# Earlier scores, a begun attention stage and six stack loads in a fused cross-attention and ternary-FFN kernel

## The chip, the cores and the metric

One core of one Trainium2 chip runs the whole program. The metric is device microseconds (us) of one execution, the median of the runs taken; lower is better. Where a profiled execution is read, times count from the start of its span.

## The reference, cut to what matters

Four sequences of 512 rows. Cross-attention with 32 heads of 16 channels: `q = layernorm(x) Wq`, `k, v = ctx Wkv`, rotary turn of q and k, softmax of `q k / 4`, weighted v, `Wout` and bias, added to x. Then an FFN on a second layer norm: weights become ternary, `sign(round(w / (mean|w| + 1e-6)))` times the mean, rows are quantised to 128 steps, gelu between the two products, added again. The scores must keep fp32 accuracy: q and k are each split in three bf16 parts, and a score is six products of parts (q0k0, q1k0, q2k0, q0k1, q1k1, q0k2) summed in one matmul over 96 stacked rows.

```python
logits = jnp.einsum('bqhd,bkhd->bhqk', q, k) * scale
w = jax.nn.softmax(logits, axis=-1)
attn = jnp.einsum('bhqk,bkhd->bqhd', w, v)
gamma = jnp.mean(jnp.abs(w))
return jnp.sign(jnp.round(w / (gamma + EPS))) * gamma
```

## The kernel before, in words

Every engine has its program written out by hand, in `xattn_ffn` (L1160); order is kept by semaphores alone.

**Projection.** Sixteen tiles of 128 rows, in steps s = 3 to 18. A step of TensorE: turn a tile of ctx and of x, turn the rotated k of the tile before, `project_k`, `project_v`, turn the rotated q, `project_q` (each product in high and low parts, L281). VectorE multiplies by the rotary tables (`rope_products`, L394 to L396) and takes rests (`take_first`, L404), ScalarE copies and splits (L466, L471), GpSimd adds and makes the third part (L502, L506). The parts go to HBM (`store_parts`, L235, twelve transfers for two tiles).

**Early scores.** The row maxima of groups 0 and 1 (a group is 4 heads of one sequence, 32 groups in all) are found within the projection: 32 single scores (`early_scores`, L672) go through one PSUM bank, each read by VectorE (`early_maxima`, L731) before the next is made. Three per step from s = 10; numbers 27 to 31 come behind the last step. Then `add_totals` (L314) and on VectorE `weigh_ffn` (L326) make the FFN's thresholds, four small operations and one more for `gamma_128`.

**Attention.** `tensor_step` (L710) s runs `scores` of group s (maxima by `row_maxima`, L736), `scores_turned` of group s - 2 (its exponentials by `exponentials`, L755), and `weigh_v` of group s - 2, a chunk late. A group's scores need its stacks: 96 rows of q parts and of k parts in SBUF, 4 KB a row, in four slots (`load_stacks`, L573). They need them whole, since `scores` waits for all of them ahead of its first matmul (L657). Group 0's first turned score waits for the last products and rests of the projection at once (L687 to L690).

**The way of a maximum.** GpSimd negates and splits a group's maxima (`split_maxima`, L765), SP turns them with a DMA (`turn_max`, L587) and loads them as two rows below the q stack (`load_max`, L594). `scores_turned` waits for that.

**SP's queue.** All DMAs are issued by SyncE's queue, in the order written. In attention, per SP step s (it falls into `tensor_step` s - 1): `turn_max(s-2)`, `load_stacks(s)`, `load_max(s-2)`, `load_weight(s)`, `pack_sums` (stores a group's sums; every other step `load_quotients`, L633), `turn_weight(s-2)`.

**GpSimd in attention.** `stage_v`, `split_maxima`, `ternarise` of an FFN weight piece (L780, three operations), `divide`.

A stack is loaded by seven transfers, the tuples being (first sixteenth of the target, part, parts):

```python
(mem.q_stack, mem.q_parts, ((0, 0, 3), (3, 0, 2), (5, 0, 1))),
(mem.k_stack, mem.k_parts, ((0, 1, 1), (1, 0, 1), (2, 0, 1), (3, 0, 3))),
```

Two other transfers matter below. `load_quotients` reads 8 blocks of 16 rows of 2 KB (L637, L638) and 8 rows of 2 KB, each repeated 16 times (`unsqueeze(1).to_broadcast([8, 16, 512])`, L639), into 128 partitions. `load_max` writes 2 partitions.

Of the kernel before, what the change touches and what calls it, by code (L numbers as in the profile page):

```python
# [16 lines left out]
HEADS, HEAD = 32, 16  # L17
# [22 lines left out]
STACK_LOADS = DMA * 7  # L40
# [63 lines left out]
class Project:  # L104
# [165 lines left out]
    def product(self, pe, out, lhs, slot, rhs, low_ready, done, high=None, low=None):  # L270

        count = rhs[0].shape[1]
        for a, b in ((0, 0), (0, 1), (1, 0)):
            if a == 1:
                pe.wait_ge(*low_ready)
# [22 lines left out]
    def project_q(self, pe, n):  # L298
# [4 lines left out]
        self.product(pe, self.in_bank[1], self.xT, n % 2, self.wq_sb, (self.x_low_ready, n + 1), self.projected[1],  # L303
                     high, low)
# [21 lines left out]
    def weigh_ffn(self, dve):  # L326
        mem = self.mem
        dve.wait_ge(self.total_ready, 1)
        dve.tensor_scalar(mem.gammas[:], self.total_bank, 1.0 / (FFN * DIM), None, ALU.mult).then_inc(self.gamma_step, 1)
        dve.wait_ge(self.gamma_step, 1)  # L330
        dve.tensor_scalar(self.gamma_eps[:], mem.gammas[:], FFN_EPS, None, ALU.add).then_inc(self.gamma_step, 1)
        dve.wait_ge(self.gamma_step, 2)
        dve.tensor_scalar(mem.limits[:, 0], self.gamma_eps[:], 0.5, None, ALU.mult).then_inc(self.gamma_step, 1)
        dve.tensor_scalar(mem.limits[:, 1], self.gamma_eps[:], -0.5, None, ALU.mult).then_inc(self.gamma_step, 1)
# [146 lines left out]

    def weight_high_too(self, pool, loaded, high, raw, ready):
# [27 lines left out]
class Attend:  # L510
# [3 lines left out]
    SINGLES = EARLY * GH * CHUNKS  # L514
    ST_BANKS = 3

    def __init__(self, nc, mem, prj, sem):
# [8 lines left out]
        self.inverse = slots(late.take(2 * SEQ), 2)  # L526
        self.v_ones = late.take(2 * CHUNKS * GH * 2 * HEAD).rearrange("p (s c h e) -> p s c h e", s=2, c=CHUNKS, h=GH)
        self.raw = slots(late.take(2 * DIM), 2)
# [41 lines left out]

    def load_stacks(self, sp, g):  # L573
        mem, slot = self.mem, g % STACK_SLOTS
# [3 lines left out]
        for stack_sb, where, runs in (  # L578
            (mem.q_stack, mem.q_parts, ((0, 0, 3), (3, 0, 2), (5, 0, 1))),
            (mem.k_stack, mem.k_parts, ((0, 1, 1), (1, 0, 1), (2, 0, 1), (3, 0, 3))),  # L580
        ):
            src = where[g].rearrange("t (d h) c -> (t d) (h c)", h=GH)
            for to, part, count in runs:
                sp.dma_start(stack_sb[to * HEAD:(to + count) * HEAD, slot].rearrange("p h c -> p (h c)"),  # L584
                             src[part * HEAD:(part + count) * HEAD]).then_inc(self.stacks_loaded[slot], DMA)
# [95 lines left out]
    def scores_turned(self, pe, g, k):  # L681
# [15 lines left out]
    def weigh_v(self, pe, g, c):  # L697
        pe.wait_ge(self.exp_done, g * 16 + GH * (c + 1))
        if c == 0:
            pe.wait_ge(self.v_staged, g + 1)  # L700
            if g == 0:
# [7 lines left out]

    def tensor_step(self, pe, s):  # L710
        turned, before = s - 2, s - 3
        for c in range(CHUNKS):
            if 0 <= turned < GROUPS:
                self.scores_turned(pe, turned, 4 * c)
            if s < GROUPS:
                self.scores(pe, s, 2 * c)
            if 0 <= turned < GROUPS:
# [8 lines left out]
            if s < GROUPS:  # L726
# [53 lines left out]
    def ternarise(self, pool, n):  # L780
        w, limits = n % 2, self.mem.limits
        if n == 0:
# [9 lines left out]
                           ).then_inc(self.ternary_ready, 1)  # L792

# [366 lines left out]
def xattn_ffn(nc, x, ctx, pos, wq, wkv, wout, bout, w_fc, w_proj, out):  # L1160
    with ExitStack() as stack:
# [5 lines left out]
        att = Attend(nc, mem, prj, sem)  # L1167
        rows = Rows(nc, mem, att, sem)
# [5 lines left out]
        def _(sp):  # L1174
# [4 lines left out]
            for s in range(TILES + 6):  # L1179
# [5 lines left out]
                if s == TILES + 4:  # L1185
                    sp.wait_ge(prj.projected[1], TILES)
                    att.load_weight(sp, w_fc, w_proj, 0)
                    att.load_weight(sp, w_fc, w_proj, 1)
                if within(s - 5, TILES) and (s - 5) % 2 == 1:
# [6 lines left out]
            for pair in range(2):  # L1196
                sp.wait_ge(prj.parts_stored[pair], PAIR_STORES * BATCH)
# [44 lines left out]
        def _(pe):  # L1242
# [7 lines left out]
            for s in range(3, TILES + 3):  # L1250
                if 2 <= s - 2 < TILES:
# [7 lines left out]
                if s >= 10:  # L1259
                    att.early_scores(pe, 3 * (s - 10))  # L1260
# [4 lines left out]
                if s >= 10:  # L1265
                    att.early_scores(pe, 3 * (s - 10) + 1)
                if within(s - 3, TILES):
                    prj.project_q(pe, s - 3)
                if s >= 10:
                    att.early_scores(pe, 3 * (s - 10) + 2)  # L1270
# [23 lines left out]
        def _(dve):  # L1294
# [17 lines left out]
            for s in range(3, TILES + 3):  # L1312
                if within(s - 4, TILES):
                    prj.rope_products(dve, s - 4, 1)
                if s > 10:
                    att.early_maxima(dve, 3 * (s - 11) + 2)
# [5 lines left out]
                if s >= 10:  # L1322
                    att.early_maxima(dve, 3 * (s - 10))
# [4 lines left out]
                if s >= 10:  # L1328
# [206 lines left out]
```

## Time and profile before

| what | us |
|---|---|
| median of 3 runs | 794.77 (794.23 to 797.53) |
| the profiled execution | 797.79 |
| its span | 795.9 |
| PE busy (matmuls; ends are modelled) | 768.5 |
| DVE busy | 674.4 |
| ACT busy | 456.1 |
| POOL busy | 341.0 |

PE is TensorE's matmul side, PEld its weight loads, DVE VectorE, ACT ScalarE, POOL GpSimd, SP SyncE; a q behind the name is the engine's queue. L12 is line 12 of the kernel before. A row of a timeline has the start, the duration, and in brackets the idle time before it with what ended that. Matmuls are pipelined, so the duration of one isn't the distance to the next.

### The profile page before, as it was taken

What the parts mean: (1) busy time and instruction counts of PE and PEld (TensorE: products, weight loads), DVE (VectorE), ACT (ScalarE), POOL (GpSimd) and SP (SyncE); (2) the same over time, 40 slices, a digit from 0 to 9 for tenths busy, and PEclk for the clock granted to TensorE, in tenths of its full rate; (3) what the DMA queues carried; (4) which work ended last, traced back from release to release, by engine and by line L of the source; (5) the groups of instructions that cost most, each with busy time, mean ns of one, the idle gap of its engine ahead of it and who ended that gap; (6) DMA issues with size and microseconds to landing.
All of it is one profiled execution on the core that took longest, in us unless ns stands there. A gap on an engine that the chain in (4) does not pass through costs nothing.

```text
span 795.9 us, 11662 instructions
## 1 busy us (share of the span) xinstructions
PE 768.5 (97%) x3812; PEld 331.6 (42%) x3812; DVE 674.4 (85%) x945; ACT 456.1 (57%) x811; POOL 341.0 (43%) x445
## 2 busy tenths in 40 slices
PE   4899999799999999999999999999999999999998
PEld 3688877233333222323322222244444444444443
DVE  7788998688888888888888888269999999898895
ACT  5677776477777777767777777734322333223430
POOL 4688777743454455445445544623222121110001
PEclk9999999699999999999999999999999999999999
DMA  8488897535577769796887996326456654555545
GB/s 288 127 216 241 256 254 184 129 109 137 147 141 152 154 158 142 152 171 149 146 155 180 171 176 137 82 57 137 107 110 144 132 106 93 108 117 87 112 87 137
DMA packets 178861, 117.22 MB, mean 147 GB/s; under 512 B 119746, under 2 KB 150514, under 8 KB 178802
## 3 DMA queue, kind: packets, MB, share of 16 engines
q1 hardware_dynamic: 178802, 116.49, 65.7%
q8 instruction: 30, 0.49, 0.3%
q14 instruction: 29, 0.24, 0.1%
HBM read 64.50 MB, written 25.43 MB: 113 GB/s over the span
## 4 chain that ended last, share of the span: by engine, by line
PE 86%; DMA 6%; DVE 3%; SPq 2%; POOL 1%; issue 1%; ACT 1%; POOLq 0%; ACTq 0%
PE banks L967 14%; PE banks L952 14%; PE banks L706 13%; PE banks L692 12%; PE banks L281 11%; PE banks L667 11%; PE banks L938 7%; DMA stack_words<-max_rows 4%; DMA max_rows<-max_parts 2%; PE banks L310 2%; SPq L584 1%; PE banks L678 1%; DVE maxima L740 1%; DMA attn_words<-in_x_dram 1%; ACT probs_words L760 1%
## 5 line engine op out<-in xcount | busy, mean ns | idle before, releaser
L760 ACT ACTIVATE probs_words<-banks 128x512 f32<-128x512 f32 x512 | 272.1, 598 | 101.7 <-PE banks L692 101.0
L740 DVE TENSOR_REDUCE maxima<-banks 128x2 f32<-128x1024 f32 x240 | 283.4, 1216 | 45.6 <-PE banks L667 45.5
L692 PE MATMUL banks<-stack_words 98*128 98x512 bf16 x512 | 175.4, 386 | 4.8 <-DMA stack_words<-max_rows 3.4
L667 PE MATMUL banks<-stack_words 96*128 96x512 bf16 x480 | 144.9, 383 | 0.0
L706 PE MATMUL banks<-probs_words,late_words 128*32 128x512 f32 x1024 | 137.3, 608 | 0.7
L952 PE MATMUL banks<-ternary_words,late_words 128*128 128x512 f16 x512 | 113.1, 380 | 0.0
L967 PE MATMUL banks<-ternary_words,stack_words 128*128 128x512 f16 x512 | 112.9, 380 | 0.0
L1130 ACT ACTIVATE probs_words<-probs_words,h_moments 128x2048 f32<-128x2048 f32 (+1 forms) x17 | 32.2, 1901 | 135.4 <-DVE h_moments L1027 135.4
L692 PEld LDWEIGHTS banks<-stack_words 98*128 98x128 bf16 x512 | 39.8, 98 | 150.0 <-ACT probs_words L760 109.9
L771 POOL TENSOR_SCALAR neg_max<-maxima 128x16 f32<-128x16 f32 x32 | 8.3, 258 | 163.0 <-DVE maxima L740 161.2
L967 PEld LDWEIGHTS banks<-ternary_words,stack_words 128*128 128x128 f16 x512 | 49.9, 98 | 64.4 <-issue 6.6
L952 PEld LDWEIGHTS banks<-ternary_words,late_words 128*128 128x128 f16 x512 | 50.0, 98 | 61.5 <-issue 1.7
L1153 POOL TENSOR_SCALAR h_powers<-h_moments 128x1 f32<-128x1 f32 x16 | 5.5, 342 | 153.4 <-DVE h_moments L1027 153.4
L667 PEld LDWEIGHTS banks<-stack_words 96*128 96x128 bf16 x480 | 47.4, 99 | 56.7 <-issue 1.9
L1124 ACT ACTIVATE probs_words<-banks,row_scale 128x512 f32<-128x512 f32 x64 | 42.3, 682 | 27.5 <-PE banks L952 27.5
L938 PE MATMUL banks<-v_words,attn_words 128*128 128x512 f32 x128 | 57.7, 593 | 0.0
L786 POOL TENSOR_SCALAR late_words<-late_words,limits 128x512 f16<-128x512 f32 x32 | 50.1, 1566 | 0.3 <-POOL late_words L791 0.2
L788 POOL TENSOR_SCALAR late_words<-late_words,limits 128x512 f16<-128x512 f32 x32 | 50.2, 1570 | 0.0
L506 POOL TENSOR_TENSOR ternary_words<-attn_words,ternary_words 128x512 bf16<-128x512 f32 x32 | 37.3, 1166 | 24.3 <-ACT ternary_words L471 23.5
L706 PEld LDWEIGHTS banks<-probs_words,late_words 128*32 128x32 f32 x1024 | 20.2, 108 | 54.9 <-ACT probs_words L760 50.3
L502 POOL TENSOR_TENSOR attn_words<-attn_words 128x512 f32<-128x512 f32 x32 | 41.2, 1290 | 2.2 <-DVE attn_words L396 2.0
L1022 DVE BATCH_NORM_STATS2 h_stats<-probs_words 128x6 f32<-128x512 f32 x64 | 39.4, 679 | 0.0
(139 smaller groups left out, 962.5 us busy)
## 6 DMA issues: line engine op xcount, KB each, us to landing
o_rows<-late_words SPq DMA_DIRECT2D x32, 256.0 KB, 3.3
k_parts<-ternary_words SPq DMA_DIRECT2D x48, 128.0 KB, 3.2
q_parts<-ternary_words SPq DMA_DIRECT2D x48, 128.0 KB, 2.5
stack_words<-q_parts SPq DMA_DIRECT2D x32, 192.0 KB, 3.1
stack_words<-k_parts SPq DMA_DIRECT2D x96, 64.0 KB, 2.7
stack_words<-k_parts SPq DMA_DIRECT2D x32, 192.0 KB, 2.7
attn_words<-in_x_dram SPq DMA_DIRECT2D x16, 256.0 KB, 4.4
probs_words<-in_L_ffn_w_fc_dram SPq DMA_DIRECT2D x16, 256.0 KB, 3.7
```

The lines of the kernel that those rows point to most:

```text
L281: mm = self.nc.tensor.matmul(out, lhs[a][:, slot, k * P:(k + 1) * P], rhs[b][:, k, :], start=(a + b + k == 0), stop=(a == 1 and k == count ...
L667: mm = self.nc.tensor.matmul(self.score_slot[j % 2][:, i], self.mem.q_stack[0:STACK, slot, head, c * P:(c + 1) * P], self.mem.k_stack[0:ST ...
L692: self.nc.tensor.matmul(self.st_bank[(g * 16 + k) % self.ST_BANKS], self.mem.k_stack[0:STACK + 2, slot, head, c * P:(c + 1) * P], self.mem ...
L706: mm = self.nc.tensor.matmul(self.pv_bank[32 * j:32 * j + 32], self.v_ones[:, g % 2, c, j, :], self.probs[:, c, j, :], start=(c == 0), sto ...
L740: dve.tensor_reduce(self.maxima[:, g % 2, 2 * j:2 * j + 2], self.score_slot[j % 2], AX.X, ALU.max).then_inc(self.scores_read, 1)
L760: act.activation(self.probs[:, c, head, :], self.st_bank[(g * 16 + k) % self.ST_BANKS], ACT.Exp, scale=1 / math.sqrt(HEAD)).then_inc(self. ...
L786: pool.tensor_scalar(self.below[:], self.raw[:, w], limits[:, 1, w:w + 1], None, ALU.is_lt).then_inc(self.cut, 1)
L788: pool.tensor_scalar(self.ternary[:, w], self.raw[:, w], limits[:, 0, w:w + 1], None, ALU.is_gt).then_inc(self.cut, 1)
L938: mm = self.nc.tensor.matmul(self.y_bank[n % 2], att.attnT[:, n // CHUNKS * KX + k, c * P:(c + 1) * P], self.wout_sb[:, k, :], start=(k == ...
L952: mm = self.nc.tensor.matmul(self.fc_bank[o], self.uT[:, n % U_SLOTS, part * KX + k], self.fcT[:, k, o], start=(k + part == 0), stop=(k == ...
L967: mm = self.nc.tensor.matmul(self.proj_bank[r], self.hT[:, r, part, k], self.projT[:, k // 2, k % 2], start=(k + part == 0), stop=(part == ...
L1124: act.activation(self.h[:, n % H_SLOTS, o * DIM:(o + 1) * DIM], self.fc_bank[o], ACT.Gelu, scale=self.row_scale[:, n % U_SLOTS]).then_inc( ...
```

## The change

- Early scores start at step 9, with 2, 3, 3, 3, 3, 4, 4, 4, 3, 3 in the ten steps; all 32 lie within the projection. The fourth of a step (in the last step the third) stands inside `project_q`, ahead of its last four matmuls.
- Attention is begun ahead of the last turn of q: the first two scores of group 2 and the first two turned scores of group 0; each of the first three turned scores waits only for what its own PSUM bank held. ScalarE takes the two exponentials between its last projection copies, and loads its table for Exp a step earlier.
- The thresholds are made on GpSimd. Its two `stage_v` and the setting of pads come earlier; group 2's maxima are split between its first two `ternarise`.
- SP: the maxima of groups 0 and 1 are turned and loaded earlier; the stacks of group 4 stand ahead of group 2's maxima; from group 5 on `load_q`, then `load_max`, then `load_k`.
- A stack takes six loads. The k stack becomes k0 three times, k1 twice, k2 once, each by one load with a repeated source; the q stack stays.

```diff
-STACK_LOADS = DMA * 7
+STACK_LOADS = DMA * 6
+    FIRST_STEP = 9
+    PER_STEP = (2, 3, 3, 3, 3, 4, 4, 4, 3, 3)
...
-    def load_stacks(self, sp, g):
+    def load_q(self, sp, g):
...
+        src = self.mem.q_parts[g].rearrange("t (d h) c -> (t d) (h c)", h=GH)
+        for to, count in ((0, 3), (3, 2), (5, 1)):
+            sp.dma_start(self.mem.q_stack[to * HEAD:(to + count) * HEAD, slot].rearrange("p h c -> p (h c)"),
+                         src[0:count * HEAD]).then_inc(self.stacks_loaded[slot], DMA)
+
+    def load_k(self, sp, g):
+        slot = g % STACK_SLOTS
+        for part, to, count in ((0, 0, 3), (1, 3, 2), (2, 5, 1)):
+            src = self.mem.k_parts[g, part].rearrange("(d h) c -> d (h c)", h=GH)
+            sp.dma_start(self.mem.k_stack[to * HEAD:(to + count) * HEAD, slot].rearrange("p h c -> p (h c)"),
+                         src.unsqueeze(0).to_broadcast([count, HEAD, GH * SEQ])).then_inc(self.stacks_loaded[slot], DMA)
...
-            pe.wait_ge(self.prj.multiplied[1], TILES)
-            for side in range(2):
-                pe.wait_ge(self.prj.rest_done[side], TILES)
+            pe.wait_ge(*((self.prj.multiplied[1], TILES), (self.prj.rest_done[0], TILES), (self.prj.rest_done[1], TILES))[k])
...
+    def begin(self, pe):
+
+        self.scores(pe, self.EARLY, 0)
+        self.scores(pe, self.EARLY, 1)
+        self.scores_turned(pe, 0, 0)
+        self.scores_turned(pe, 0, 1)
...
             for s in range(GROUPS + 3):
-                if 1 <= s - 2 < GROUPS:
+                if s == 2:
+                    for pair in range(2):
+                        sp.wait_ge(prj.parts_stored[pair], PAIR_STORES * BATCH)
+                if s == 3:
+                    att.load_stacks(sp, STACK_SLOTS)
+                    att.turn_max(sp, 2)
+                    att.load_max(sp, 2)
+                if 3 <= s - 2 < GROUPS:
                     att.turn_max(sp, s - 2)
-                if STACK_SLOTS <= s < GROUPS:
-                    att.load_stacks(sp, s)
-                if 1 <= s - 2 < GROUPS:
+                if STACK_SLOTS + 1 <= s < GROUPS:
+                    att.load_q(sp, s)
+                if 3 <= s - 2 < GROUPS:
                     att.load_max(sp, s - 2)
+                if STACK_SLOTS + 1 <= s < GROUPS:
+                    att.load_k(sp, s)
...
             prj.turn_rotated(pe, TILES - 1, 0)
-            att.early_scores(pe, 27)
+            att.begin(pe)
             prj.turn_rotated(pe, TILES - 1, 1)
-            for i in range(28, att.SINGLES):
-                att.early_scores(pe, i)
...
             prj.take_first(dve, TILES - 1, 0)
-            att.early_maxima(dve, 27)
             prj.sum_ffn(dve)
-            att.early_maxima(dve, 28)
+            att.row_maxima(dve, 2, 0)
             prj.take_first(dve, TILES - 1, 1)
-            for i in range(29, att.SINGLES):
-                att.early_maxima(dve, i)
-            prj.weigh_ffn(dve)
...
+            att.set_pads(pool, 1)
+            att.stage_v(pool, 1)
+            prj.weigh_ffn(pool)
+            pool.tensor_scalar(rows.gamma_128[:], mem.gammas[:], 1 / Q_B, None, ALU.mult).then_inc(rows.gamma_set, 1)
+            att.ternarise(pool, 0)
+            att.split_maxima(pool, 2)
+            att.ternarise(pool, 1)
```

## Rows read from the trace of the kernel before

**Rows 1.** The page: line 4's shares of the chain, and the turned scores' group.
```profile
PE 86%; DMA 6%; DVE 3%; SPq 2%; POOL 1%; issue 1%; ACT 1%; POOLq 0%; ACTq 0%
L692 PE MATMUL banks<-stack_words 98*128 98x512 bf16 x512 | 175.4, 386 | 4.8 <-DMA stack_words<-max_rows 3.4
```

**Rows 2.** Busy time by stretch: span, length, PE, PEld, DVE, ACT, POOL (count), clock, DMA share, GB/s.
```profile
59.63:66.70 7.07, 7.07 (x39) 5.95 (x39) 5.61 (x14) 5.60 (x13) 5.90 (x8) 1.00 0.61 161
...
97.48:105.23 7.75, 7.75 (x42) 6.17 (x42) 7.29 (x16) 5.59 (x13) 5.86 (x8) 1.00 0.99 282
138.30:147.57 9.27, 4.40 (x17) 1.88 (x17) 6.60 (x12) 3.69 (x5) 4.97 (x6) 0.73 0.76 183
147.57:161.96 14.39, 14.39 (x58) 4.03 (x58) 10.08 (x12) 8.21 (x15) 10.59 (x11) 0.70 0.34 64
161.96:173.31 11.35, 11.35 (x66) 3.48 (x65) 9.93 (x9) 8.47 (x17) 5.32 (x7) 1.00 0.55 160
...
298.52:311.05 12.53, 11.51 (x65) 3.32 (x64) 11.12 (x11) 9.10 (x18) 6.55 (x8) 1.00 1.15 158
```

**Rows 3.** Timeline of the handover on DVE and POOL, and of PE's weighing in the next step.
```profile
138.53 0.69 DVE L394 TENSOR_TENSOR attn_words<-banks,ternary_words 128x512 f32<-128x512 f32 x1 [1.06 <-PE banks L281]
...
139.97 1.26 POOL L502 TENSOR_TENSOR attn_words<-attn_words 128x512 f32<-128x512 f32 x1 [0.60 <-DVE attn_words L396]
...
140.40 0.68 DVE L404 TENSOR_TENSOR attn_words<-banks,ternary_words 128x512 f32<-128x512 f32 x1
...
165.76 1.06 PE L706 MATMUL banks<-probs_words,late_words 128*32 128x512 f32 x8
```

**Rows 4.** PE's busy time and clock before and after the clock falls.
```profile
139.00:142.50 3.50, 1.43 (x8) 1.00 0.81 211
142.60:156.20 13.60, 10.90 (x29) 0.50 0.52 118
```

**Rows 5.** Timeline of SP's queue and of PE while group 0's stacks are loaded.
```profile
63.58 1.81 SPq L584 DMA_DIRECT2D stack_words<-k_parts  x4
...
66.10 0.38 PE L310 MATMUL banks<-ident,attn_words 128*128 128x128 f32 x2
```

**Rows 6.** Timeline of SP's queue in an attention step; PE's first score of the next.
```profile
371.57 1.12 SPq L592 DMA_TRANSPOSE max_rows<-max_parts  x1
372.80 1.44 SPq L584 DMA_DIRECT2D stack_words<-q_parts  x3
374.28 1.81 SPq L584 DMA_DIRECT2D stack_words<-k_parts  x4
376.14 0.70 SPq L596 DMA_DIRECT2D stack_words<-max_rows  x1
...
380.62 0.59 PE L667 MATMUL banks<-stack_words 96*128 96x512 bf16 x2
```

**Rows 7.** DMA issues: KB each, us from issue to landing where it is told.
```profile
stack_words<-k_parts SPq DMA_DIRECT2D x96, 64.0 KB, 2.7
...
late_words<-inverse_rows SPq DMA_DIRECT2D x16, 256.0 KB
...
max_rows<-max_parts SPq DMA_TRANSPOSE x32, 2.4
stack_words<-max_rows SPq DMA_DIRECT2D x32, 8.0 KB
```

**Rows 8.** Timeline of SP's queue: the quotients of a pair.
```profile
228.56 0.65 SPq L638 DMA_DIRECT2D late_words<-o_rows  x1
229.25 0.61 SPq L639 DMA_DIRECT2D late_words<-inverse_rows  x1
```

**Rows 9.** Busy time while they move; the last two columns are DMA share and GB/s.
```profile
232.50:233.50 1.00, 1.00 (x6) 0.43 (x5) 1.00 (x3) 1.00 (x3) 1.00 (x2) 1.00 0.51 193
```

**Rows 10.** The chain of waits in order of time, in a step behind quotients.
```profile
301.03 5.18 DMA max_rows<-max_parts
306.23 4.77 DMA stack_words<-max_rows
```

More of the change, by code:

```diff
@@ L274, in product @@
             if a == 1:
+                if between is not None:
+                    self.att.early_scores(pe, between)
                 pe.wait_ge(*low_ready)
@@ L526, in __init__ @@
         self.inverse = slots(late.take(2 * SEQ), 2)
+        self.raw = slots(late.take(2 * DIM), 2)
         self.v_ones = late.take(2 * CHUNKS * GH * 2 * HEAD).rearrange("p (s c h e) -> p s c h e", s=2, c=CHUNKS, h=GH)
-        self.raw = slots(late.take(2 * DIM), 2)
         self.below = late.take(DIM // 2, F16)
@@ L569, in __init__, with early_of @@
         self.divided = sem("divided")
-    def load_stacks(self, sp, g):
-        mem, slot = self.mem, g % STACK_SLOTS
+    def early_of(self, s):
+        at = s - self.FIRST_STEP
+        if not 0 <= at < len(self.PER_STEP):
+            return []
+        first = sum(self.PER_STEP[:at])
+        return list(range(first, first + self.PER_STEP[at]))
+    def load_q(self, sp, g):
+        slot = g % STACK_SLOTS
         for pair in range(2):
@@ L577, in load_stacks @@
         need(sp, self.st_ready, (g - STACK_SLOTS + 1) * 16)
[L578 to L585, printed above, removed]
+        src = self.mem.q_parts[g].rearrange("t (d h) c -> (t d) (h c)", h=GH)
[3 more added lines that the diff above has]
+    def load_k(self, sp, g):
+        slot = g % STACK_SLOTS
+        for part, to, count in ((0, 0, 3), (1, 3, 2), (2, 5, 1)):
+            src = self.mem.k_parts[g, part].rearrange("(d h) c -> d (h c)", h=GH)
+            sp.dma_start(self.mem.k_stack[to * HEAD:(to + count) * HEAD, slot].rearrange("p h c -> p (h c)"),
+                         src.unsqueeze(0).to_broadcast([count, HEAD, GH * SEQ])).then_inc(self.stacks_loaded[slot], DMA)
+    def load_stacks(self, sp, g):
+        self.load_q(sp, g)
+        self.load_k(sp, g)
     def turn_max(self, sp, g):
@@ L712, in tensor_step @@
         for c in range(CHUNKS):
-            if 0 <= turned < GROUPS:
+            begun = s == self.EARLY and c == 0
+            if 0 <= turned < GROUPS and not begun:
                 self.scores_turned(pe, turned, 4 * c)
-            if s < GROUPS:
+            if s < GROUPS and not begun:
                 self.scores(pe, s, 2 * c)
-            if 0 <= turned < GROUPS:
+            if 0 <= turned < GROUPS and not begun:
                 self.scores_turned(pe, turned, 4 * c + 1)
@@ L725, in tensor_step @@
                 self.scores_turned(pe, turned, 4 * c + 3)
-            if s < GROUPS:
+            if s < GROUPS and not begun:
                 self.scores(pe, s, 2 * c + 1)
@@ L1250, in _ @@
             for s in range(3, TILES + 3):
+                early = att.early_of(s)
                 if 2 <= s - 2 < TILES:
@@ L1258, in _ @@
                     prj.project_k(pe, s - 3)
-                if s >= 10:
-                    att.early_scores(pe, 3 * (s - 10))
+                if len(early) > 2:
+                    att.early_scores(pe, early[0])
                 if 1 <= s - 3 < TILES:
@@ L1321, in _ @@
                     prj.take_first(dve, s - 4, 0)
-                if s >= 10:
-                    att.early_maxima(dve, 3 * (s - 10))
+                if len(early) > 2:
+                    att.early_maxima(dve, early[0])
                 if s < TILES:
@@ L1411, in _ @@
                     prj.normalise(act, s - 1)
+                if s == TILES + 3:
+                    att.exponentials(act, 0, 0)
                 if within(s - 4, TILES):
@@ L1419, in _ @@
                     prj.first_part(act, s - 4, 1)
+                    if s == TILES + 3:
+                        att.exponentials(act, 0, 1)
                     prj.second_part(act, s - 4, 1)
+                if s == TILES + 2:
+                    act.preload_act_table(ACT.Exp)
             for s in range(2, GROUPS + 3):
-                for k in range(16):
+                for k in range(2 if s == 2 else 0, 16):
                     if within(s - 2, GROUPS):
```

84 lines of the change are left out of this document (48 added, 36 removed).

## The prediction

> **What bounds the kernel now.** I read the page first. TensorE holds 86% of the chain that ended last, DMAs 6% [rows 1]. The page's group of turned scores shows where DMAs enter: of 4.8 us that TensorE idles ahead of them, 3.4 us are waits for `load_max`. Then the table by stretch [rows 2]. A projection step takes 7.07 us without early scores and 7.75 us with three, TensorE busy throughout, VectorE 7.29 us of it. A steady attention step takes 11.35 us, again TensorE throughout, with VectorE at 9.93, ScalarE at 8.47 and GpSimd at 5.32. Between the two lies the handover: from the end of the last product (138.3) to the start of the second attention step (161.96) are 23.7 us, with TensorE busy 4.40 us of the first 9.27, while the five late scores go back and forth with VectorE. There the clock falls: behind 3.5 us in which TensorE was busy 1.43, the granted clock is half for 13.6 us [rows 4]. So two things can be won, the handover and 3.4 us of waits; a step of attention can only be lost.
>
> **The handover.** The work that remains behind the last product: VectorE's rotary products start 0.2 us after it, GpSimd's sum ends at 141.23, 2.9 us after it [rows 3]. Then one behind another a turn on TensorE, ScalarE's copy, VectorE's rest (0.68), a turned score and two exponentials: six operations, 0.65 each by the rest's row, 3.9 us. The first weighing of v starts so 6.8 us after the product. In a steady step it starts 3.8 us in (165.76 against 161.96), 7.55 us before the step's end. Sum 14.35 against 23.7: 9.3 us to win at full clock. `turn_rotated` of q stands behind `begin` on TensorE, whose second turned score waits for VectorE's rest of k: products from 138.53, rest 0.68, so 140.6, before GpSimd's 141.23; nothing lost.
>
> Against it stands what moves into the projection. Before the last product's end lay 26 early scores, now 32: six more by (7.75 - 7.07) / 3 = 0.23 us, 1.4 us. Two of the steps with four maxima keep their statistics: VectorE 7.29 + 0.68 = 7.97 of 7.98 us. The score inside `project_q` then waits for the maximum before it; I take 0.3 us each, 0.6 us (bounds 0 and 1.4, two maxima). The first early score of step 9 meets the stacks of group 0: TensorE reaches it at 66.4, and the k loads are issued from 63.58 [rows 5]. Its wait hangs on the k loads: 63.58 + 2.7 - 0.2 + 5.5 = 71.6 by the price below, less the 0.4 taken off there, a wait of 4.8 us; about 1.0 if they move as now (the third, issued near 64.6, lands 2.7 later). At full clock 9.3 - 1.4 - 0.6 - 4.8 leaves a gain of 2.5 us. The clock may fall in that wait or in the handover; it costs step one now at most 14.39 - 11.35 = 3.0 us. I take 1.5 and 0.5 for the later landing of group 4's stacks, on which the turn of group 2's maxima is queued: handover 0.5 us won.
>
> The thresholds leave VectorE for GpSimd, ahead of its first `ternarise`; GpSimd idles half of each step [rows 2], and only the loads of weight pieces wait for it. I cost this, the pads, the two early `stage_v` and ScalarE's earlier table load at nothing. Without that cover it is the four operations' length on GpSimd once, about 1 us.
>
> **The six loads.** This is the term that decides. A step's q and k loads are all issued one step ahead of use. In the step shown [rows 6] the turn is issued at 371.57, q at 372.80, k at 374.28, `load_max` at 376.14, and the scores that need all the loads start at 380.62. The change puts `load_max` (0.70) ahead of k; k is issued from 375.03. That alone costs nothing: a k load lands 2.7 us after its issue [rows 7], by 379.
>
> But the new k loads have a repeated source, three blocks of 16 rows and two blocks of 16 rows, the repeat outermost. What does an outermost extent of 8 do now? The quotients' two transfers [rows 8] have one, and while they move, the 16 DMA engines are busy to 0.51, 193 GB/s in all [rows 9]: eight engines, 23.7 GB/s each. The table of issues gives no landing for these, nor for `load_max` with its 2 partitions, while all that have 16 or more rows outermost have one [rows 7]: the profile counts sixteen engines' completions, and these have fewer. So I expect three engines for the first k load and two for the second, and the second on two of the same, as the two quotient transfers share theirs. On those two lie 32 rows of 4 KB, 131 KB each, 131 / 23.7 = 5.5 us, where sixteen engines take 0.2 us for a 64 KB load.
>
> The Trainium skill, page DMA: Bandwidth & Descriptors, section "Why a DMA increments its semaphore by 16 and not by 1", says that a DMA uses the largest number of engines up to 16 that divides the outermost extents of both sides, and the lowest-numbered ones; the trace agrees for the extent 8 with its share of 0.51. By the rule the sum is the forecast; without it, the rival below.
>
> The price: 375.03 + 2.7 - 0.2 + 5.5 = 383.0 against 380.62, a stall of 2.4 us. The median of 2.7 includes waiting behind other transfers, so I take 2.0. Behind quotients the turn itself takes 5.18 us [rows 10], not 2.4, which puts k later; but a stretched step gives the quotients more time to drain, so I take 2.0 there too. Bounds 0.9 (landing 1.1 earlier) and 3.5. Groups 5 to 31 are 27: 54 us (24 to 95). The 3.4 us of waits for `load_max` go, since its rows land first. What is late next is k; scores, maxima and the next turn follow it, so nothing later absorbs the stall.
>
> **Sum.** 797.8 (profiled execution, span 795.9) - 0.5 - 3.4 + 54 = 847.9. That execution lies 3.0 above the median of the runs, 794.77; I forecast **845 us**.
>
> **Rivals.** (1) **The repeated loads spread over all sixteen engines**, as one with 16 or more rows does. Then k lands by 379, the stack wait of step 9 is 1.0, the handover wins 9.3 - 1.4 - 0.6 - 1.0 = 6.3 us, less up to 3 for the clock, and some 2 of the 3.4 us of waits go: 794.8 - 6.3 - 2 = 786.5 to 790, faster. It decides where the k loads land less than 5.6 us after issue. For it: their target has 48 and 32 rows; against: the quotients' target has 128 and they use eight. (2) **The two repeated loads use different engines**: 64 KB on each, 2.8 us. Odd steps then land at 380.3 and stall no more, even ones by under 1 us: 794.8 - 5 + 13 x 0.5 = 796, no change. Against it: the quotients' share of eight with two transfers in flight. (3) **The clock halves in the stalls**: 2 us of idle in a step resemble the 1.43 of 3.5 of rows 4. Half the clock for 3 us costs 1.5 us a step, in half of the steps 20 us: 865. For it, the fall seen; against, the step from 298.52, with 1.02 of 12.53 us idle, stays at full clock [rows 2].
>
> **Chances.** Forecast 0.65, (3) 0.12, (1) 0.18, (2) 0.05. Slower by over 0.5% (which is what a measurement of this kernel can tell from no change) 0.77, within 0.05, faster 0.18. The forecast's own range is 815 to 886, from the bounds of the stall. Since slower holds less than 8 in 10, the range reaches into (1): 789 to 886.
>
> **What would show it.** Right: the issue rows of the two repeated k loads give no landing; TensorE's waits ahead of L667's successor name the stacks, some 2 us a step; steps of 13 us; DMA share near 2/16 while k moves; TensorE idle near 66 us. The handover shown right: the second attention step starts some 14 us after the last product. Wrong: steps stay at 11.35, k lands within 3 us with a landing told. Then (1) holds and the end is below 791.

## The result, and the profile after

The changed kernel takes **879.17 us** (median of 6 runs, 875.69 to 883.23); the kernel before took 796.85 on the same chip (794.23 to 798.62). The ratio is 1.104, with an interval of 1.100 to 1.108: slower by 82 us. The forecast was 845, with a range of 789 to 886. Direction and place were right; the sum is 34 us short, and the way it was counted was wrong, as the experiments show. One run of the last experiment, the profiled one, took 991.37 us at a granted clock of 0.755; its median below is over the other five runs, and its trace isn't read.

The page of the profiled execution (880.1 us, span 878.3): shares of the chain that ended last, the groups of scores and of turned scores (busy, mean ns | idle before, releaser), and the issues of DMAs (KB each, us to landing where it is told).

```profile
PE 66%; DMA 16%; SPq 7%; DVE 3%; POOL 3%; ACT 2%; issue 2%; POOLq 0%; DVEq 0%; ACTq 0%
...
L689 PE MATMUL banks<-stack_words 96*128 96x512 bf16 x480 | 151.9, 399 | 50.8 <-DMA stack_words<-k_parts 50.8
L712 PE MATMUL banks<-stack_words 98*128 98x512 bf16 x512 | 183.6, 403 | 4.0 <-DVE attn_words L401 1.6
...
stack_words<-q_parts SPq DMA_DIRECT2D x32, 192.0 KB
stack_words<-k_parts SPq DMA_DIRECT2D x32, 192.0 KB
...
stack_words<-k_parts SPq DMA_DIRECT2D x32, 128.0 KB
stack_words<-k_parts SPq DMA_DIRECT2D x32, 64.0 KB
max_rows<-max_parts SPq DMA_TRANSPOSE x32, 3.3
```

Against [rows 1], TensorE's share of the chain falls from 86% to 66% and DMA's rises from 6% to 16%. The scores, which waited for nothing worth a place among the rows of before, idle 50.8 us, all for the k loads; of the waits for the maxima's rows ahead of L712 one of 0.8 us is left. Against [rows 7], the k loads have no landing any more, and the turn of the maxima takes 3.3 us instead of 2.4 (with plain k loads, experiment 1, it takes 3.0, so the repeated loads are not all of that).

The table by stretch of the changed kernel, with the columns of [rows 2]: step 9; handover up to group 0's first turned score; attention's first step; three steady steps; and one microsecond in which TensorE stands still.

```profile
62.41:80.95 18.54, 9.67 (x41) 7.60 (x39) 6.21 (x13) 5.73 (x13) 7.34 (x9) 0.72 0.80 200
...
151.60:153.14 1.54, 1.31 (x10) 0.59 (x7) 1.50 (x4) 1.28 (x2) 1.37 (x5) 1.00 0.09 28
153.14:168.25 15.11, 13.23 (x59) 4.02 (x60) 9.58 (x11) 9.83 (x18) 9.53 (x13) 0.77 0.66 167
208.78:220.12 11.34, 11.34 (x65) 3.42 (x64) 9.93 (x9) 8.46 (x17) 5.32 (x7) 1.00 0.36 103
220.12:236.41 16.29, 13.10 (x65) 3.46 (x64) 10.41 (x10) 8.52 (x17) 5.37 (x7) 0.90 0.79 115
236.41:247.76 11.35, 11.35 (x66) 3.42 (x64) 9.93 (x9) 8.46 (x17) 5.32 (x7) 1.00 0.39 100
...
222.00:223.00 1.00, 0.00 (x0) 0.00 (x0) 0.00 (x0) 0.00 (x0) 0.86 (x3) 1.00 0.17 54
```

The steps don't take 13 us each, as forecast. In most pairs one of 11.35 alternates with one of 16 to 19. In the last row little but k moves. Of its 54 GB/s, 45 go in packets of 4 KB, which is a row of k; summed from the trace, these keep 2.0 of the 16 DMA engines busy, with 22 GB/s each, near the 23.7 of the quotients' eight [rows 9]. Most of the rest of the share of 0.17 is short packets of 256 bytes.

The trace also keeps the completions that each load counts on its semaphore. A group's six loads make 71 of them. Where every load has 16 or more rows outermost, each makes 16; that is 48 for q and 16 for the last k load, so 7 are left for the two repeated loads. The quotients' two loads, with 8 outermost, make 9 each, and the maxima's rows, with 2, make 3: one more than the outermost extent. Seven is so 3 + 1 and 2 + 1, three engines and two.

Where the 82 us lie, by the first turned scores of groups 1 and 31: up to group 1 6.3 us (168.25 against 161.96), from there to group 31 76.1 us (423.1 against 347.0), behind group 31 nothing (287 to the span's end in both).

The chain of waits through one such stall, in order of time (start, duration, what):

```profile
208.98 1.24 DVE maxima L770
...
211.29 1.13 SPq L614
212.53 0.52 SPq L595
214.01 0.70 SPq L618
214.76 0.71 SPq L602
215.51 0.61 SPq L602
216.17 7.47 DMA stack_words<-k_parts
223.69 0.98 PE banks L689 x2
```

The maxima of group 5 are found, GpSimd splits them, SP turns them (L614), issues q, the maxima's rows and k of group 7; k lands 9 us after its first issue, and only then do the scores of group 7 start. Their maxima release the turn that stands ahead of group 9's k. So this is a ring that goes round once in two steps.

### The profile page after: what moved, and what is told of

Read it like the earlier page. It is cut to its first block, busy times and chain, and to the rows that moved or that the text cites. A ratio compares the mean times of both kernels' runs of the same rounds, so it can differ in the third digit from the quotient of the medians.

```text
span 878.3 us, 11628 instructions
## 1 busy us (share of the span) xinstructions
PE 797.2 (91%) x3812; PEld 335.5 (38%) x3812; DVE 676.4 (77%) x941; ACT 457.7 (52%) x811; POOL 341.3 (39%) x450
## 4 chain that ended last, share of the span: by engine, by line
PE 66%; DMA 16%; SPq 7%; DVE 3%; POOL 3%; ACT 2%; issue 2%; POOLq 0%; DVEq 0%; ACTq 0%
PE banks L1000 13%; PE banks L985 13%; DMA stack_words<-k_parts 12%; PE banks L728 9%; PE banks L712 8%; PE banks L283 8%; PE banks L689 7%; PE banks L971 6%; DMA max_rows<-max_parts 3%; SPq L602 2%; DVE maxima L770 2%; SPq L595 1%; PE banks L312 1%; SPq L618 1%; SPq L614 1%
## 5 line engine op out<-in xcount | busy, mean ns | idle before, releaser
L689 PE MATMUL banks<-stack_words 96*128 96x512 bf16 x480 | 151.9, 399 | 50.8 <-DMA stack_words<-k_parts 50.8
L712 PE MATMUL banks<-stack_words 98*128 98x512 bf16 x512 | 183.6, 403 | 4.0 <-DVE attn_words L401 1.6
L728 PE MATMUL banks<-probs_words,late_words 128*32 128x512 f32 x1024 | 147.9, 652 | 0.7
L712 PEld LDWEIGHTS banks<-stack_words 98*128 98x128 bf16 x512 | 40.4, 99 | 159.7 <-ACT probs_words L790 102.5
```

Of the source, the lines that this page charges most:

```text
L689: mm = self.nc.tensor.matmul(self.score_slot[j % 2][:, i], self.mem.q_stack[0:STACK, slot, head, c * P:(c + 1) * P], self.mem.k_stack[0:ST ...
L712: self.nc.tensor.matmul(self.st_bank[(g * 16 + k) % self.ST_BANKS], self.mem.k_stack[0:STACK + 2, slot, head, c * P:(c + 1) * P], self.mem ...
L728: mm = self.nc.tensor.matmul(self.pv_bank[32 * j:32 * j + 32], self.v_ones[:, g % 2, c, j, :], self.probs[:, c, j, :], start=(c == 0), sto ...
```

## The experiments

All kernels but one start from the changed one. "Attention" is the time between the first turned scores of groups 1 and 31; "waits" is TensorE's idle time in it that ends with a stack's load or a row of maxima; "half clock" the time in it at a granted clock of 0.50; "k" the median from the first k issue to the landing of the group's last load. The last three are summed from the trace. "Before" on the same chip was 797.0 us for experiments 1 to 4, 797.6 for 5 and 7 to 9, 795.59 for 6 and 10; the ratios are to these. Where a row says "one run", there is no interval.

| kernel | us | ratio, interval | attention | waits | half clock | k |
|---|---|---|---|---|---|---|
| before | 796.85 | | 347.0 | 3.4 | 0 | 5.02 |
| changed | 879.17 | 1.104, 1.100 to 1.108 | 423.1 | 51.6 | 61.4 | 9.17 |
| plain k loads | 791.34 | 0.993, 0.990 to 0.996 | 345.1 | 1.8 | 0 | 4.12 |
| before, repeated loads | 869.91 | one run | 412.3 | 44.4 | 51.2 | 9.41 |
| repeat inside | 795.57 | 0.997, 0.994 to 1.000 | 350.4 | 6.4 | 0 | 4.50 |
| second load split | 826.4 | one run | 374.8 | 22.7 | 13.7 | 7.17 |
| filled stalls | 878.62 | 1.102, 1.099 to 1.104 | 421.2 | 26.5 | 17.1 | 9.22 |
| k first | 911.58 | 1.146, 1.143 to 1.149 | 460.3 | 81.8 | 85.3 | 12.5 |
| plain, filled handover | 788.29 | 0.989, 0.987 to 0.991 | 343.8 | 0.8 | 0 | 4.11 |
| plain, from step ten | 789.04 | 0.990, 0.987 to 0.992 | 345.1 | 2.3 | 0 | 4.11 |
| plain, maxima behind k | 792.44 | 0.993, 0.990 to 0.995 | 345.4 | 2.3 | 0 | 4.06 |
| plain, ten and filled | 787.58 | 0.991, 0.989 to 0.992 | | | | |

**1. The change without its repeated loads.**

```diff
-STACK_LOADS = DMA * 6
+STACK_LOADS = DMA * 7
...
-        for part, to, count in ((0, 0, 3), (1, 3, 2), (2, 5, 1)):
-            src = self.mem.k_parts[g, part].rearrange("(d h) c -> d (h c)", h=GH)
+        src = self.mem.k_parts[g].rearrange("t (d h) c -> (t d) (h c)", h=GH)
+        for to, part, count in ((0, 1, 1), (1, 0, 1), (2, 0, 1), (3, 0, 3)):
...
-                         src.unsqueeze(0).to_broadcast([count, HEAD, GH * SEQ])).then_inc(self.stacks_loaded[slot], DMA)
+                         src[part * HEAD:(part + count) * HEAD]).then_inc(self.stacks_loaded[slot], DMA)
```

> The changed kernel with the k stack loaded by the four unrepeated loads of the kernel before (seven loads a stack); everything else, load_max ahead of k included, stays. Theory A (a source repeated outermost puts the two k loads on three and two of the same DMA engines, and that is the whole loss): k lands some 2.7 us after issue, attention steps go back to 11.35 us, the total is 786 to 793 us, ratio to before 0.985 to 0.997. Rival B (k is late because it now stands behind the turn and load_max on SP's queue): steps stay over 12.5 us, the total over 830.

791.34 us, faster than before by 0.4 to 1.0%. Its page has landings for all stack loads, its table by stretch shows step 9, attention's first two steps, and the time at half clock:

```profile
stack_words<-q_parts SPq DMA_DIRECT2D x32, 192.0 KB, 3.1
stack_words<-k_parts SPq DMA_DIRECT2D x96, 64.0 KB, 2.2
stack_words<-k_parts SPq DMA_DIRECT2D x32, 192.0 KB, 2.7
```

```profile
62.83:71.18 8.35, 7.41 (x41) 5.95 (x39) 6.20 (x13) 5.73 (x13) 6.91 (x9) 1.00 0.74 214
...
143.40:158.57 15.17, 13.29 (x59) 4.06 (x59) 9.57 (x11) 9.83 (x18) 9.54 (x13) 0.77 0.66 164
158.57:169.93 11.36, 11.36 (x66) 3.43 (x65) 9.93 (x9) 8.48 (x17) 9.27 (x10) 1.00 0.40 108
145.90:152.70 6.80, 5.88 (x18) 1.44 (x19) 3.11 (x4) 4.07 (x9) 5.62 (x11) 0.50 0.85 194
```

So the repeated loads cost the changed kernel 88 us (879.17 against 791.34), and everything else in the change is worth some 5. The steps of attention are back at 11.36, and step 9 takes 8.35 instead of 18.54.

**2. The repeated loads alone, in the kernel before.** `load_stacks` of before with the changed kernel's six loads and nothing else:

```diff
-            (mem.k_stack, mem.k_parts, ((0, 1, 1), (1, 0, 1), (2, 0, 1), (3, 0, 3))),
...
+        for part, to, count in ((0, 0, 3), (1, 3, 2), (2, 5, 1)):
+            src = mem.k_parts[g, part].rearrange("(d h) c -> d (h c)", h=GH)
...
+                         src.unsqueeze(0).to_broadcast([count, HEAD, GH * SEQ])).then_inc(self.stacks_loaded[slot], DMA)
```

> The kernel before with only the six loads put in: three q loads as they were, three k loads with a repeated source, in before's order (k ahead of load_max). Theory A: k lands some 9 us after issue, near 12.5 us into the step, and load_max, issued behind it on the same engines, lands with it: steps of 13 to 14 us on average, 855 to 880 us. Rival B (the order is at fault, not the loads): within 1% of 797.

869.91 us in the one run, 73 above before. The wait has another name, since `load_max` stands behind k in this queue:

```profile
PE banks L692 <- DMA stack_words<-max_rows: 44.4, 16, 3.6
```

So the loads by themselves, without anything else of the change, cost 73 of the 88 us that they cost in it, and the order of the queue decides in which wait they end. Where the other 15 lie is only in part seen: in the change they cost 78 us of attention (423.1 against 345.1), here 65.

**3. The same repeat, 16 channels outermost.** Six loads again, each source read in another order: the 16 channels outermost, the repeat inside. The bytes and rows are the same; the order of the rows in the stack changes for q and k alike, so a score sums the same products.

```diff
-                         src[0:count * HEAD]).then_inc(self.stacks_loaded[slot], DMA)
+                         self.mem.q_parts[g, 0:count].rearrange("t (d h) c -> d t (h c)", h=GH)
+                         ).then_inc(self.stacks_loaded[slot], DMA)
...
-                         src.unsqueeze(0).to_broadcast([count, HEAD, GH * SEQ])).then_inc(self.stacks_loaded[slot], DMA)
+                         src.unsqueeze(1).to_broadcast([HEAD, count, GH * SEQ])).then_inc(self.stacks_loaded[slot], DMA)
```

> The changed kernel with six loads and the same repeated reading, but the rows of a block interleaved so that the extent of 16 stands outermost and the repeat inside it (q's rows are interleaved likewise). Theory A: all sixteen engines move every load, k lands about 2.7 us after issue, total as in the run with plain k loads, 786 to 793. Rival C (reading the same HBM rows two and three times is what is slow): k lands after some 9 us as in the changed kernel, total over 860.

795.57 us: above the expected 786 to 793, but 84 us below the changed kernel. k lands 4.50 us after its first issue, and the page tells a landing:

```profile
stack_words<-k_parts SPq DMA_DIRECT2D x32, 192.0 KB, 3.2
```

It isn't the repeat that costs, but which extent stands outermost. The Trainium skill, page DMA: Bandwidth & Descriptors, section "Why a DMA increments its semaphore by 16 and not by 1", has the number of engines as the largest up to 16 that divides the outermost extents of both sides; outermost 3 and 2 (9.17 us) against 16 (4.50 us) agrees with it. In this kernel all six loads of a group make 16 completions each. The 4 us by which it lies above plain loads (the intervals overlap) are in attention (350.4 against 345.1), 6.4 us of waits at eight groups of about 0.8 us; why k lands 0.4 us later than with plain loads isn't shown.

**4. Do the two repeated loads share their engines?** Only the second repeated load becomes two plain ones.

```diff
-        for part, to, count in ((0, 0, 3), (1, 3, 2), (2, 5, 1)):
+        for part, to, count in ((0, 0, 3), (1, 3, 1), (1, 4, 1), (2, 5, 1)):
```

> The changed kernel with the two-fold repeated load of k1 made by two plain loads; the three-fold load of k0 stays repeated outermost (seven loads). Theory A (the second load queues behind the first on the same engines, 16 rows of 4 KB each): k lands about 3 us earlier than in the changed kernel, 6 us after issue; the stall of every second step falls from 3.5 us to under 1 and the clock holds: 790 to 805 us. Rival D (the two loads use different engines, and the three-fold one alone takes the 9 us): unchanged, 865 to 880.

826.4 us, above the 790 to 805 expected, but k lands after 7.17 instead of 9.17 us. Had the two loads been on different engines, taking away the second, which is issued 0.75 us behind the first (215.51 against 214.76 above), would have won little more than that. The completions say the same, though the page names no engines: in each of the 27 groups of the changed kernel exactly eight of the 71 come later than 5.0 us behind the first k issue, the first load's three, the second's two, and of the last load's sixteen those of three engines. On different engines they would be ten. In this run a group makes 100 completions, six loads of 16 and the first load's 4. The size of the gain says more. k lands 2.0 us earlier in each of 27 groups, and the waits fall by 28 us (50.8 to 22.7): about 2.0 in every second step, not in each. Another 20 of the 48 us won in attention go with the half clock, 13.7 us instead of 61.4.

**5. The clock in the stalls.** TensorE's time in the changed kernel's attention can be told apart: 47 us more waits than before (50.8 - 3.4), and 28.7 us that are left, which go with 61.4 us at half clock, spread over 13 of the stalls, 3.4 or 6.8 us each. TensorE's waits for k, in us in total, times, and the longest:

```profile
PE banks L689 <- DMA stack_words<-k_parts: 50.8, 18, 4.9
```

Is the half clock a cost of its own? The stalls are filled with work that is thrown away:

```diff
+    FILL = 7
...
+        if j == 0 and g > STACK_SLOTS:
+            need(pe, self.scores_read, (g - self.EARLY) * 2 * GH + j - 1)
+            for i in range(self.FILL):
+                self.nc.tensor.matmul(self.score_slot[0][:, i % 2], self.mem.q_stack[0:STACK, (g - 1) % STACK_SLOTS, i % GH, 0:P],
+                                      self.mem.k_stack[0:STACK, (g - 1) % STACK_SLOTS, i % GH, :], start=True, stop=True)
         if j == 0:
             pe.wait_ge(self.stacks_loaded[slot], (g // STACK_SLOTS + 1) * STACK_LOADS)
```

> The changed kernel, repeated k loads and all; ahead of the first score of each group from 5 on, TensorE makes seven scores over again (512 columns of the stack of the group before, overwritten by the real ones), 1.5 us at full clock, while the stack is on its way. Theory (clock): of the 76 us that attention lost, some 28 are the clock, which falls in stalls of 3 to 4 us; the wait itself is a loop over two steps (maxima of group s - 2, turn, k loads, scores of group s) that takes some 25.8 us a pair of steps at full clock, where a pair without stalls takes 22.7. Two times 1.5 us of added work fit into a pair's 3.1, so added work costs next to nothing, the idle stretches shrink to under 2 us, the 61 us of half clock in attention go below 20, and the kernel gets faster by added work: 850 to 862 us. Rival (waits alone): the clock is a by-product and the time is set by when k lands; then the end stays at 875 to 885 whatever the clock shows. Second rival (work is work): TensorE is what bounds even here, and 27 x 1.5 = 40 us come on top: 905 to 920.

878.62 us: within the rival's 875 to 885. Two steps of it by stretch, TensorE's waits, and the turn of the maxima on its page:

```profile
222.55:235.76 13.21, 13.03 (x72) 4.02 (x71) 10.41 (x10) 8.52 (x17) 5.33 (x7) 1.00 0.66 117
235.76:248.88 13.12, 13.03 (x73) 4.02 (x71) 10.21 (x9) 8.52 (x17) 5.33 (x7) 1.00 0.67 121
```

```profile
PE banks L695 <- DMA stack_words<-k_parts: 25.1, 18, 3.1
```

```profile
max_rows<-max_parts SPq DMA_TRANSPOSE x32, 4.2
```

The clock came back (17.1 us at half instead of 61.4), the waits halved, TensorE had 27 x 1.5 = 41 us more to do, and the end didn't move. My theory foretold the clock and missed the time. Where nothing else is in the way a pair of steps does get shorter: from one split of maxima to the next but one it is 26.1 us here (212.19 to 238.25) and 27.6 in the changed kernel (211.26 to 238.90). But over all pairs it is 28.2 against 28.4: the turn of the maxima takes 4.2 us instead of 3.3 in the median, and the four longest steps behind group 4 (17.2 to 17.8 us) each stall behind a turn of 5.4 to 6.1 us, of groups 10, 16, 24 and 28. So what a pair wins is lost again to later turns. Why they are later stays open: of 26 turns, 12 are issued while k of the step before is still moving, and in the changed kernel 14. Filling this way gives none of the 28.7 us back. Whether the clock alone would, without 41 us of added work, no run shows.

**6. k at the head of the queue's turn.** If k stands in a ring of two steps, moving it out of the ring should help.

```diff
+                if STACK_SLOTS + 1 <= s < GROUPS:
+                    need(sp, att.st_ready, (s - STACK_SLOTS + 1) * 16)
+                    att.load_k(sp, s)
                 if 3 <= s - 2 < GROUPS:
                     att.turn_max(sp, s - 2)
                 if STACK_SLOTS + 1 <= s < GROUPS:
                     att.load_q(sp, s)
                 if 3 <= s - 2 < GROUPS:
                     att.load_max(sp, s - 2)
-                if STACK_SLOTS + 1 <= s < GROUPS:
-                    att.load_k(sp, s)
```

> The changed kernel, repeated k loads and all, with the k loads of group s at the head of SP's turn, ahead of the turn of group s - 2's maxima, from group 5 on. Theory (one loop over two steps): a group's stack waits for the maxima of two groups before, so what k is late costs once a pair of steps, and moving k ahead of the turn takes it out of that loop; k is issued 5 us and more earlier against its use. What is late then is the turn, which lands behind k on the same DMA engines and holds the turned scores; that lateness is smaller, 1 to 2 us a pair. The k_parts waits fall from 50.8 us below 15, waits for the maxima's rows come up to 20 us, and the end is 812 to 840. Rival (the queue is full): turn, q, k and the quotients together take the two lowest DMA engines 13 to 14 us a step, whatever their order; then steps stay at 13.5 to 14 us on average and the end at 865 to 885.

911.58 us, worse than both expectations. The waits, the turn's landing on the page, and a stretch of SP's queue:

```profile
PE banks L712 <- DMA stack_words<-max_rows: 81.6, 27, 6.6
```

```profile
max_rows<-max_parts SPq DMA_TRANSPOSE x32, 8.3
```

```profile
234.91 1.87 SPq L602 DMA_DIRECT2D stack_words<-k_parts  x3
236.91 1.14 SPq L614 DMA_TRANSPOSE max_rows<-max_parts  x1
238.16 1.44 SPq L595 DMA_DIRECT2D stack_words<-q_parts  x3
245.11 0.68 SPq L618 DMA_DIRECT2D stack_words<-max_rows  x1
```

k is no longer waited for (none of the waits names it in attention). The turn now lands 8.3 us after its issue instead of 2.4 [rows 7] to 3.0 (plain k loads), and SP stands from 239.6 to 245.1 until it has, with everything else behind it. I had put the turn's lateness at 1 to 2 us; it is 6. The Trainium skill, page DMA: Bandwidth & Descriptors, section "Queues, rings and completion order", says that a queue's transfers are taken in order on each DMA engine; the turn's 8.3 us behind k and 2.4 without it agree. What stands behind the repeated loads in the queue pays for them; of the three orders tried (the change's, before's, k first) none hides them.

**7. The handover's clock.** In the kernel of the first experiment the second attention step starts 16.7 us after the last product (141.86 to 158.57), 6.8 of them at half clock. Eleven scores over again fill the idle places.

```diff
         self.scores(pe, self.EARLY, 1)
+        pe.wait_ge(self.early_read, self.SINGLES)
+        self.fill(pe, 2)
         self.scores_turned(pe, 0, 0)
+        self.fill(pe, 2)
         self.scores_turned(pe, 0, 1)
+        self.fill(pe, 2)
+
+    def fill(self, pe, count):
+        for i in range(count):
+            self.nc.tensor.matmul(self.early_bank, self.mem.q_stack[0:STACK, 1, i % GH, 0:P],
+                                  self.mem.k_stack[0:STACK, 1, i % GH, :], start=True, stop=True)
...
             prj.turn_rotated(pe, TILES - 1, 1)
-            pe.wait_ge(att.early_read, att.SINGLES)
+            att.fill(pe, 5)
```

> The kernel of the first experiment (the change with four plain k loads) with eleven scores made over again in the idle places behind the last product: 2 ahead of the first turned score, 2 ahead of the second, 2 behind it, 5 behind the last turn of q, some 0.2 us each at full clock. Theory (clock): the 6.8 us at half clock from 145.9 on cost about 3 us; with TensorE kept at work they go, and group 1 starts 1.5 to 3 us earlier behind the last product than the 16.9 us it does there; end 788 to 790. Rival (dependencies): the handover is set by the chain from VectorE over ScalarE to the exponentials, the half clock lies beside it, and the added scores only push it back: group 1 starts at 16.9 us or later, end 791 to 795.

788.29 us. The table by stretch from the last product on, and the first weighing of v in the timeline (start, duration):

```profile
141.67:143.24 1.57, 1.57 (x11) 0.81 (x9) 1.52 (x4) 1.31 (x2) 1.40 (x5) 1.00 0.42 69
143.24:156.05 12.81, 12.35 (x68) 4.42 (x67) 9.59 (x12) 9.66 (x19) 9.53 (x13) 1.00 0.66 162
```

```profile
148.29 1.06 PE L728 MATMUL banks<-probs_words,late_words 128*32 128x512 f32 x8
```

The clock stays full, and the second step starts 1.57 + 12.81 = 14.38 us after the last product. Here, unlike in the stalls, filling wins back what the half clock cost, 2.3 us: TensorE's own work stands on the path, and no late transfer behind it takes the gain.

**8. Early scores from step ten**, with plain k loads.

```diff
-    FIRST_STEP = 9
-    PER_STEP = (2, 3, 3, 3, 3, 4, 4, 4, 3, 3)
+    FIRST_STEP = 10
+    PER_STEP = (3, 3, 3, 4, 4, 4, 4, 4, 3)
```

> The kernel of the first experiment with the early scores from step 10 on, as before the change, in nine steps of 3, 3, 3, 4, 4, 4, 4, 4, 3. Theory: the only cost of step 9 was the wait for the stack of group 0 (0.9 us); it goes, two more steps with four scores give some 0.3 us each back, and group 1 starts within 1 us of 158.6, end 789 to 793. Rival (VectorE): with five steps of four maxima VectorE falls behind, 0.5 us and more in each, and group 1 starts 1 to 3 us later; end 792 to 796.

789.04 us. The wait for group 0's stack is gone; steps with four scores take 8.0 to 8.2 us against 7.76 with three. From the end of the first `project_q` to that of the last it is 118.1 us instead of 119.2: 1.0 us, more than the theory's 0.9 less two times 0.3. Group 1 starts at 155.62, 3.0 earlier than 158.57, where the theory had it within 1 us; another 0.8 us lie ahead of the first tile, and the clock fell in the handover for 3.4 us instead of 6.8.

**9. Maxima's rows behind k**, as before the change, with plain k loads.

```diff
                 if STACK_SLOTS + 1 <= s < GROUPS:
                     att.load_q(sp, s)
+                if STACK_SLOTS + 1 <= s < GROUPS:
+                    att.load_k(sp, s)
                 if 3 <= s - 2 < GROUPS:
                     att.load_max(sp, s - 2)
-                if STACK_SLOTS + 1 <= s < GROUPS:
-                    att.load_k(sp, s)
```

> The kernel of the first experiment with the two rows of maxima issued behind the k loads, as before the change. Theory: the order of the queue was worth the 3.4 us of waits for these rows; they return, the 1.8 us of waits for k go, and attention is 1.5 to 3.5 us longer than 345.1; end 792 to 795. Rival: six q and k loads in front instead of seven let the rows land in time anyway, attention stays at 345 to 346, end 790 to 792.

792.44 us, attention 345.4 against 345.1, where the theory had it 1.5 to 3.5 longer. (The rival's text miscounts: this kernel has seven loads in front, as before.) Waits for the maxima's rows of 2.3 us return, and those for k of 1.8 us go. The order exchanges one wait for another; it is worth 0.3 us in the trace, which no run tells from nothing.

**10. The three together**: plain k, from step ten, filled handover.

> Plain k loads, early scores from step ten, and the eleven scores made over again in the handover: the three findings together. Theory: they add up, since they lie in different places: 1.0 us behind the kernel with the filled handover alone, group 1 starting 14.4 us after the last product; end 786 to 788. Rival: from step ten the clock fell in the handover for 3.4 us only, so the filling is worth less here; end 788 to 790.

787.58 us, about 1% below before and 10% below the changed kernel. It can't be told from the filled handover alone (788.29); only its time is used here.

## Why the prediction was right, and where it was not

**The decisive term was seen, for the right reason.** Outermost extents of 3 and 2, no landing told, 2.0 of 16 engines busy with k, the second load on the first one's engines: the trace of the change and the experiments with plain loads, the repeat inside and the split load bear these out. Rival (1), with 786.5 to 790, describes what the change would do with plain loads: 791.3.

**The price of a k load was mis-sized.** Forecast: landing 8.0 us after issue, with 23.7 GB/s an engine; measured 9.17. The rate holds where k is nearly alone: from 6 to 8 us behind the first issue, over the 27 groups, the packets of 4 KB move 46.0 GB/s on 1.95 engines, 23.6 each. From 3 to 6 us, while other transfers are under way, it is 19 for each engine busy with them. The split load took off 2.0 us, where 64 KB at 23.6 GB/s are 2.8, so not all of the landing goes by the bytes.

**The step that failed is "Groups 5 to 31 are 27: 54 us".** It puts a stall of 2.0 into every step, as if each were late against a fixed plan. But the turn that stands ahead of k follows from the scores of two groups before: k is late once in a ring of two steps, 13.5 times. By my own 2.4 us that would have been 32 us. Measured, a clean pair takes 27.6 us (220.12 + 16.29 - 208.78) where before took two times 11.35: 4.9 us late instead of 2.4. Of these 2.5 more, 1.2 are k's later landing (9.17 against 8.0), and the rest goes with the half clock (with the stalls filled a clean pair takes 26.1). The mean over 13.5 pairs is 76.1 / 13.5 = 5.6: in five of the long steps the half clock lasts 6.8 us, and they take 17.3 to 18.8 us, where the eight with 3.4 us of it take 15.8 to 16.9. So there are 14 long stalls of 3.5 us in the mean, and four short ones, for 27 of 2.0: the errors nearly cancel in the waits (50.8 against 54), and the time at half clock makes up the rest. That 879 lies inside the range is in part luck: its upper end, 886, stood for 3.5 us in every step, and no term of it for the clock. The alternation, 11.35 and 16 to 19, follows from the ring: a stalled step delays the next one's need, but not its loads.

**Rival (3) came true in its mechanism and not as a sum.** I had kept the clock apart, with 20 us and a chance of 0.12. The clock did halve, in 13 stalls, and a stall lasts 2.8 us in the mean and up to 4.9, not 2. But in the filled stalls, with most of the full clock back, the end stayed: there its time is not a sum that is simply added to the waits.

**The handover.** Before, the last product ends at 138.50 by the trace, not 138.3, so the second step stood 23.5 us behind it, and the six operations at the row's 0.68 are 4.1 us, not 3.9. Forecast at full clock 14.35 us from the last product to the second attention step; with the idle places filled 14.38, the first weighing after 6.6 (6.8 forecast). With plain loads and nothing filled 16.7, so the clock's share is 2.3 where I took 1.5. In the changed kernel the gain was lost earlier: step 9 waited 8.9 us, not 4.8, since the first stack landed at 75.5 instead of 71.2, and TensorE ran at half clock for 10.2 us around it; 18.54 us instead of 7.07. So the part up to group 1 lost 6.3 us instead of winning 0.5. With plain loads that wait is 0.9 (1.0 forecast), and the part wins 3.4.

**"The 3.4 us of waits for `load_max` go"**: with plain loads they do, but waits for k of 1.8 us take the place of half of them; the order alone is worth 0.3. Thresholds on GpSimd, pads and the early stages cost nothing that the trace shows: attention with plain loads is 1.9 us shorter than before.

## What to carry to other kernels

Before fewer, larger transfers are written, look at the outermost extent of both sides; where the profile tells no landing for a transfer, ask whether fewer engines than all carry it, or another transfer on its semaphore. In this kernel the repeat belonged inside an extent of 16, not around it. Where a transfer is late, find the ring in which it stands and count its lateness once per turn of the ring, with whatever else waits on the same engines. Before time at half clock is counted as a cost of its own, fill such a gap once, and see whether the end moves: in the handover it did, in the stalls not.

## What the runs showed of the hardware

Two engines with k's rows of 4 KB moved 23.6 GB/s each when little else was under way, the quotients' eight with rows of 2 KB 23.7 [rows 9], and the former 19 when other transfers were; which engines they are stays open. A load with 3, 2 or 8 outermost counts 4, 3 or 9 completions, and one with 16 or more counts 16. The q loads, which the change leaves as they were, lose their landing on the page wherever k's are repeated around 16 rows, and have one, 3.1 us, with plain k loads; both count on one semaphore. And the granted clock fell again and again, mostly 27 to 31 us apart, in the longer stalls (of 18 waits the mean is 2.8 us, the longest 4.9), each time for 3.4 or 6.8 us, though TensorE could be busy for all of the step before (11.34 of 11.34 us in the row of 208.78, ahead of the fall at 223.8).
